# A fused two-layer block on one core: new orders of the steps on all five engines

## The reference

```python
# block 1, time mixing and channel mixing
x = ln(x); xn = ln(x); xk, xv, xr = three mixes of xn and xn shifted by one token
k = exp(min(xk @ Wk, 60)); v = xv @ Wv; r = xr @ Wr            # 512 wide
wk, wkv = running sums over the tokens of k and k*v, with a decay per channel
x = x + (sigmoid(r) * wkv / (wk + eps)) @ Wo
xn = ln(x); x = x + sigmoid(xr @ cWr) + silu(xk @ cWk) @ cWv
# block 2, a soft tree: 255 gates, 256 leaf probabilities, their values
gate = sigmoid(x @ Wq.T @ routers.T); ret = leaf_probs(gate) @ leaf_values @ Wout.T + b
# block 3, causal attention, 16 heads of 8, rms norm, rope
out = softmax(q k^T / sqrt(8) + causal) @ v @ Wo
# block 4, 16 routed experts, the best 2 of a softmax, and 2 shared ones
out = u + sum_e gate_e * (u @ Wr_e.T + br_e) + shared
```

## Time and profile before

| | us |
|---|---|
| median of 3 runs (lowest to highest) | 2122.58 (2116.55 to 2122.89) |
| the profiled execution, its time | 2123.6 |
| the profiled execution, its span | 2121.8 |
| PE busy in the span | 1803.8 |
| DVE busy | 1556.5 |
| ACT busy | 1008.4 |
| POOL busy | 926.7 |
| mean granted TensorE clock | 0.91 |

### The profile page before, as it was taken

One profiled execution on the slowest core, in us unless ns is written; L12 is line 12 of the kernel. 1 busy time (PEld: TensorE's weight loads), 2 busy tenths in 40 slices (PEclk: granted clock), 3 DMA queues, 4 the chain that ended last, 5 costly groups with the idle time before them and its releaser, 6 DMA issues.

```text
span 2121.8 us, 33790 instructions
## 1 busy us (share of the span) xinstructions
PE 1803.8 (85%) x12141; PEld 1110.8 (52%) x12141; DVE 1556.5 (73%) x3386; ACT 1008.4 (48%) x1997; POOL 926.7 (44%) x1160
## 2 busy tenths in 40 slices
...
GB/s 90 1 5 45 1 20 33 7 45 12 46 12 45 1 44 14 12 46 12 46 12 46 12 46 1 25 33 12 45 12 45 12 46 1 43 9 10 43 12 6
DMA packets 64617, 53.34 MB, mean 25 GB/s; under 512 B 6019, under 2 KB 63171, under 8 KB 64451
## 3 DMA queue, kind: packets, MB, share of 16 engines
...
## 4 chain that ended last, share of the span: by engine, by line
PE 37%; DVE 37%; ACT 12%; issue 6%; POOL 4%; DMA 3%; SPq 1%; ACTq 0%; DVEq 0%; POOLq 0%
PE bank L870 34%; DVE rmax L741 10%; DVE wkb L688 4%; DVE ksum L675 4%; DVE tree L651 4%; PE bank L866 4%; ACT prob L462 3%; DMA qh<-maxT 3%; DVE kvsum L680 2%; DVE prob L821 2%; DVE rmax L738 2%; POOL rstd L341 2%; DVE stats L642 2%; DVE kvb L651 1%; ACT xd L468 1%
## 5 line engine op out<-in xcount | busy, mean ns | idle before, releaser
L462 ACT ACTIVATE prob<-bank 128x512 f32<-128x512 f32 x640 | 353.8, 594 | 132.5 <-PE bank L870 123.1
L741 DVE TENSOR_REDUCE rmax<-bank 128x1 f32<-128x512 f32 (+2 forms) x768 | 351.5, 501 | 48.5 <-PE bank L870 48.1
L428 POOL TENSOR_TENSOR prob<-xdT,spread 128x512 f32<-128x512 f32 x128 | 162.2, 1267 | 393.3 <-ACT spread L462 393.3
L870 PE MATMUL bank<-qh,kh 75*128 75x512 bf16 (+3 forms) x1024 | 270.0, 318 | 67.0 <-ACT prob L462 44.9
L870 PE MATMUL bank<-kh,qh 72*128 72x512 bf16 (+3 forms) x1024 | 279.0, 320 | 31.1 <-DVE rmax L741 13.6
L462 ACT ACTIVATE spread<-bank 128x512 f32<-128x512 f32 x128 | 76.4, 597 | 476.2 <-PE bank L870 476.2
L870 PE MATMUL bank<-wexpT,prob 128*128 128x128 f32 x2048 | 288.8, 285 | 0.0
L870 PEld LDWEIGHTS bank<-wexpT,prob 128*128 128x128 f32 x2048 | 255.3, 195 | 35.5 <-issue 24.0
L870 PEld LDWEIGHTS bank<-qh,kh 75*128 75x128 bf16 x1024 | 103.6, 101 | 254.9 <-ACT prob L462 176.5
L688 DVE RECIPROCAL wkb<-wkb 128x512 f32<-128x512 f32 x64 | 213.7, 3338 | 0.0
L870 PE MATMUL bank<-maskTb,identb 128*128 128x128 bf16 x1024 | 202.3, 228 | 0.0
...
## 6 DMA issues: line engine op xcount, KB each, us to landing
...
```

The source lines that it names most:

```text
L428: raised(pool.tensor_tensor(ug[:, e % 4, :], xdT[:, :], spread[e // 2 % 2][:, :], ALU.mult), "ug_side")
L462: raised(act.activation(dst, src, func, **kw), signal)
L741: last = dve.tensor_reduce(rmax[:, j, h:h + 1], S[n % 2][:, col:col + (j + 1) * P], AX_X, ALU.max)
L870: return pe.matmul(out_, w, x, start=start, stop=stop, **kw)
```

## The change

Only the five strings of `ORDER` are other ones. The steps, their instructions, the semaphores and the values waited for are the same; each engine does the same work in another order. The diff is a table of tokens; its line for SP reads:

```diff
     sp="""
-        7:heads 7:max_rows 5:load 9:store
+        2:heads 0:load 2:max_rows 4:store
     """,
```

More of the change, by code:

```diff
@@ L51 @@
     sp="""
-        7:heads 7:max_rows 5:load 9:store
+        2:heads 0:load 2:max_rows 4:store
     """,
     pool="""
-        1:root1 2:res 2:cmr_sig 4:root6 2:cmr_sum 2:root3 4:gate_rest 4:gate_lo 4:u1 4:u3 4:u5 4:u7 1:wk0 4:u9 1:r_sig0 4:u11 4:u13 2:root4 2:root_rms
-        4:u15 1:r_sig1 1:wk1 1:gated0 1:rwkv0 2:rope_sum0 2:rope_sum1 2:rest0 1:r_sig2 1:gated1 1:rwkv1 2:rest1 1:wk2 1:gated2 1:wk3 1:rwkv2 1:r_sig3
-        1:gated3 1:rwkv3 4:root7 2:part_lo0 0:root0 2:part_lo1 1:root2 0:x1_gain 0:x1_bias
+        4:u5 4:u7 4:u9 0:root0 4:u11 1:r_sig0 4:u13 4:u15 1:gated0 1:wk0 1:r_sig1 1:wk1 4:root7 1:rwkv0 1:gated1 2:root4 2:root_rms 1:r_sig2 1:rwkv1 1:wk2
```

52 lines of the change are left out of this document (27 added, 25 removed).

## The result

| | before | after |
|---|---|---|
| median (lowest to highest), us | 2121.96 (2116.55 to 2122.89) | 2224.85 (2212.56 to 2232.13) |
| the profiled execution, its span | 2121.8 | 2230.3 |
| mean granted TensorE clock | 0.91 | 0.858 |

The ratio is 1.0485, with a 95% interval of 1.0427 to 1.0542: the changed kernel is slower, where 2069 us was forecast and the range ended at 2125. All ratios in this document compare executions that lie within 1.5% of the fastest of their kernel; one of the four of rows_only and three of the ten of dummies_idle_back lie above, and the medians hold them.

The account below looks back on a forecast made before the run. No engine was full; a per-batch ring of waits was taken as the bound, its row stage DVE's. Turn 5.0 + 38.1 + 16.6 + 55.6 = 115.3; span 2121.8 - 18 - 35 = 2068.8, forecast 2069 us, range 2030 to 2125.

Parts of the forecast that it names:

- Score stage, 38.1: Stretch of a turn from maxT's landing to the first head DMA; predicted to go from 38.7 to 38.1 us.
- Head window, 16.6: From the first head DMA to row0's matmul; predicted to fall from 23.3 to 16.6 us, row0 then waiting for the DMA.
- Row stage, 55.6: Stretch from row0's matmul until the maxT step; predicted to grow from 50.8 to 55.6 us.
- moved work (+2.9): Net DVE work put between the rows by the new order, predicted to add 2.9 us to the row stage.
- new waits (+1.9): DVE waits in the row stage, 1.3 us of them at row3, predicted to add 1.9 us over today's idle.
- it is DVE's: Claim that DVE limits the row stage, being busy 48.99 of 52.00 us there in the kernel before.
- The clock as a rival, 61 and 17%: Half clock makes PE bind the row stage: stage 61, turn 121, time 2149 us; chance 17%.
- `maxT`, 5.0: Step of each turn between row stage and score stage; predicted to stay at 5.0 us, filled by experts 12 to 15.
- Filling, -18: Time before the first ring; predicted 18 us shorter, with batch 0's first row near 203.
- Draining, 0: Time after the last ring; predicted to change by 0, within 5 us.
- Scans apart, the second rival: Scans no longer collide with POOL's products, ksum at 1.2 instead of 2.0: turn 112.4, time 2029 us; chance 15%.
- rings: Per-batch cycles, each a turn, predicted to go from 117.8 to 115.3 us; fourteen of them save 35 us.

Follow-up runs that it names:

- rows_only: The changed kernel with two PE steps moved, shared from ahead of cmr to behind gT and xnT from behind gb1 to behind gb0; 2195.3 us.
- dummies_idle_back: dummies_both with xnT alone moved on PE, from behind gb1 to right ahead of row11; 2115.8 us, 0.9964 of the kernel before.
- before_fill_root7: The kernel before with two unread products ahead of xbT, and root7 moved on POOL from behind rwkv3 to ahead of r_sig2; 2121.4 us.
- fill_heads: The changed kernel with five matmuls per turn that nobody reads added on PE, two ahead of xn2T and three ahead of row0; 2178.7 us.
- heads_shared: fill_heads with the real step shared moved on PE from ahead of cmr to behind gT; 2101.1 us.
- dummies_both: fill_heads with further unread products on PE ahead of row10, row11 and gb1; 2105.7 us.
- dummies_rows: The changed kernel with unread products on PE only ahead of row10, row11 and gb1, none in the head window; 2137.2 us.

## Why the prediction was wrong, point by point

- **Score stage, 38.1.** Measured 38.1. Right in size, but not for its reason: before_fill_root7 shows that the 3.08 us wait of the earlier trace rows had `read_out` behind it and was worth 0.2. The wait at `norm_rms` was there, 1.06 us in the turn shown where 2 were expected.
- **Head window, 16.6.** The heads are issued 0.03 us after the last score, row0 runs at 819.21, 17.0 after the issue, put down to `kh<-part`. The mean is 17.6 - 0.75 = 16.85. Right. PE idles 7.8 us of the 17.00 in the turn shown, where some 6 were expected.
- **Row stage, 55.6: the step that failed.** It came out at 65.6 by the table, which is 66.4 as the prediction cuts it, from row0's matmul. At full clock it is 54.6 to 54.8 by the table (fill_heads, heads_shared, dummies_both), 55.4 to 55.6 by the prediction's cut, so the sum of moved work (+2.9) and new waits (+1.9) was right. What failed is "it is DVE's": that DVE goes on binding the stage, with the half clock priced at one wait at row3. PE fell to half clock twice, 26.1 us of it in a stage, and bound the stage there; at 0.4 us of time for each that is the 10.8 us.
- **The clock as a rival, 61 and 17%.** Its mechanism is the first half of what happened: PE idles for the DMA, the clock falls, PE binds. Its doubling of the 7 us of the earlier trace rows was right too: the first stretch is 13.7 us long (815.7 to 829.4). But it ends ahead of row5; alone it gives a row stage of 58.1 (dummies_rows), 0.8% slower than before, not 61. What the rival had no term for is the second stretch, from 843.0, behind PE's waits for DVE: it adds 7.5 us where the first adds 3.3. The rival's chance was set by the argument "the DVE work per row is more than PE's", which holds only at full clock. What it said of `y0` and `cmv` did not happen: `y0` didn't wait.
- **`maxT`, 5.0.** 5.9, from 5.6 to 7.2: 0.8 a turn that the sum had at nothing.
- **Filling, -18.** -22.0. Batch 0's first row is at 198.10, not 203.
- **Draining, 0.** +0.8.
- **Scans apart, the second rival.** `ksum` went from 1.839 to 1.736 us, `kvsum` from 1.500 to 1.296, POOL's `wkb` product from 1.400 to 1.203. The means fell by 0.1 to 0.2, where that rival wanted 0.8 for two of the `ksum`; and where the clock was half DVE did not bind the row stage.
- **The sum.** -22.0 + 15 x 8.65 + 0.8, against -18 - 35. Batch 0 to 14 are 15 rings, not the 14 that the prediction counted, which is 2.5 us. At the 116.2 us of a turn at full clock the forecast would have been off by 0.9 a turn.

The sentence on the Trainium skill (TensorE: Matmul & The Clock Gate, HAM oscillation — how this bites in real kernels) was the right warning, and the trace of after agrees with it: the wait for the heads (3.80 us in the turn shown) comes back each turn, and so does the half clock behind it, which fill_heads takes away in 9 of 13 turns. The second stretch stands behind waits of 0.62, 0.43 and 0.24 us. The Trainium skill (TensorE: Matmul & The Clock Gate, A second HAM failure mode: psum-queue depth-cycling) tells of a kernel whose short idles between groups of matmuls, as it goes round its banks, make the clock fall again and again. 836 to 843 of after, PE busy 5.46 of 7 us in such waits, agrees with it.
